# One pass of a decoder layer on Trainium2: in the last steps of the attention part VectorE makes norms and copies, weights come in order of use, pads go out on two queues

## The chip, the cores and the metric

The kernel runs on one core of one Trainium2 chip. The metric is the time of one execution on the device in microseconds (us). Engines are named as in the profile: PE (TensorE), DVE (VectorE), ACT (ScalarE), POOL (GpSimd) and SP (SyncE, which here only issues DMAs); PEld is PE's loading of weights.

## What is computed

A decoder layer with its norms behind each part, on x of 32 batches x 256 rows x 256 columns, all float32:

```python
x = _layernorm(x + _L0_attn_ref(x, Wq, Wk, Wv))               # 16 heads of 16, one k and v for all heads
x = _layernorm(x + _L0_xattn_ref(x, ctx, ctx, mask, W1, b1, W2, b2))   # 120 rows of context per batch
x = _layernorm(x + _L0_ffn_ref(x, Wg, W1, b1, Wo, bo))        # 8 experts, the two best per row
# in the last: comb holds the two best gate scores of a row, scaled to a sum of 1
for e in range(E):
    h = einsum('btd,hd->bth', x, W1[e]) + b1[e]
    a, b = split(h, 2)
    out = out + (einsum('bth,dh->btd', a * sigmoid(b), Wo) + bo) * comb[..., e:e + 1]
```

W1 has 8 experts of 1024 x 256, so one expert's weights are 1 MB.

## The kernel before

The program has three parts that follow each other.

**Attention** (function `attention`) is a software pipeline over the 32 batches, B = 32. A step t has 16 slots, u = 0 to 15; in each step the engines work on different stages of up to eight batches: t itself (projections), t-1 (maxima of the scores), t-3 (scores, exponentials, products with v), t-4 (transposes of attention's output, its sum with x, the statistics of norm 1), t-5 (norm 1, cross attention), t-6 (norm 2, the gate), t-7 (slots of the rows in the experts' lists, and POOL's indirect DMAs that write the rows there). Steps 0 to 31 bring in a batch each; steps 32 to 38 only drain. Every engine has its own program, written out by hand by slots, and works through it strictly in that order; semaphores tie the engines to each other. So an instruction that waits holds everything behind it on its engine.

The stages that matter here, for a batch b, with their lines:

- Step b+4: PE transposes attention's output in two halves, in slots 8 and 10 (`att_transpose`, L536, into the bank `psA`); DVE takes reciprocals and products (L849, L855), POOL adds x (L447), DVE makes statistics and moments (L833, L839). POOL then makes reciprocal root and shift (`rstd`, L408, L409, L411, L413).
- Step b+5: ACT applies norm 1 (L713, slot 0), PE transposes it (L563, slot 1), ACT copies that out of `psA` (L736, slot 2), PE multiplies with the keys (L579), DVE adds the mask and takes the maximum (L924, L928), ACT makes the exponentials (L759), PE transposes them (L612), ACT copies (L766), PE multiplies with the context (L628) and DVE finishes y2 (L1000, slot 14).
- Step b+6: DVE makes the moments of y2, POOL `rstd`, ACT norm 2 (L713, slot 4), PE transposes (L587), ACT copies out of the bank `psB` (L749, slot 6), PE scores the gate (L601), DVE works out the two best experts (L933 and what follows) and PE counts the rows per expert (L636 to L640).
- Step b+7: DVE makes the slots (L900, L907, L912), and POOL issues four indirect DMAs of rows (`dispatch`, L417).

The last steps also prepare the second part. SP loads the experts' weights in step 35, when the room of the probabilities is free (L288, `load_experts`), eight DMAs of 1 MB in the order of experts 0 to 7. ACT rounds each to `w1_hi` (`round_w1`, L684) and DVE makes the rest `w1_lo` (`split_w1`, L80), both in the order 4, 5, 6, 7, 0, 1, 2, 3 (`W1_ORDER`). Where these stand in the slots is set by two tables, (step, slot):

```python
rounds = {(B + 3, 15): W1_ORDER[0:2], (B + 4, 0): W1_ORDER[2:3], (B + 4, 7): W1_ORDER[3:4],
          (B + 4, 12): W1_ORDER[4:6], (B + 5, 7): W1_ORDER[6:7], (B + 5, 12): W1_ORDER[7:8]}
splits = {(B + 4, 3): 2, (B + 4, 6): 1, (B + 5, 3): 3}
```

**Experts** (function `experts`): DVE works out tables from the counts (L1367 to L1384): which rows and which expert each tile of 128 rows has. SP copies a pad of 128 rows behind each expert's list (L1161, eight DMAs), and then loads tiles (L1171). DVE makes the remaining pieces of `w1_lo` and `wo_lo` (L1388). PE waits for the tables and for all eight pieces; then a loop runs over 136 tiles: transposes (L1273), twelve matmuls (L1249, L1250, L1253), and on DVE, ACT and POOL the gating and the write of the result rows (L1405, L1412, L1416, L1329, L1212).

**Combination**: 32 pairs of tiles are read back, summed, multiplied with Wo, normed and stored.

## Time and profile before

| | |
|---|---|
| median of 3 executions | 1451.99 us (1448.6 to 1452.24) |
| the profiled execution, its own time | 1452.34 us |
| its span in the profile | 1449.7 us |
| busy: PE, DVE, ACT, POOL | 1272.7, 1129.4, 755.5, 639.0 us |
| steps 33 to 38 and the tables (754.1 to 864.4 us) | 110.3 us |
| tiles of the experts (864.4 to 1281 us) | about 417 us |

The profile describes one execution. A busy time counts an engine at work, the granted clock (PEclk) is the share of full speed at which PE was let run: 1.00 is 2.4 GHz, 0.50 is 1.2 GHz. Times of instructions are from the start of the span.

### The profile page before, as it was taken

Reading aid. Unit: us, or ns where it says so; the run is one execution under the profiler, and the core shown is the slowest. Engines: PE = TensorE matmul, PEld = TensorE weight load, DVE = VectorE, ACT = ScalarE, POOL = GpSimd, SP = SyncE. Lnnn points to the kernel's source line nnn. Section 1 sums busy time; section 2 is a strip of 40 time slices with the busy share of each in tenths; the row PEclk is TensorE's granted clock in tenths of the full one; section 3 lists DMA queues with packets and bytes.
Section 4 is the critical chain, followed back from the end, with each engine's and each line's share of the span. In section 5 each row is a group of like instructions: output and inputs, shape, how many; then the busy total and the mean of one; then the engine's idle time right before and its main releaser. Section 6 shows DMA issues by size and latency. Waiting matters only on the chain.

```text
span 1449.7 us, 29965 instructions
## 1 busy us (share of the span) xinstructions
PE 1272.7 (88%) x7668; PEld 895.3 (62%) x7669; DVE 1129.4 (78%) x3085; ACT 755.5 (52%) x1743; POOL 639.0 (44%) x1004
## 2 busy tenths in 40 slices
PE   6888999999999999999987429999999999968886
PEld 4443555655655555555543317888888888858786
DVE  1456788888888888888874567888888888859998
ACT  1125677777777777777777522222222222214444
POOL 3011244454455445445444343333333333348886
PEclk8999999999999999999999559999999999989999
DMA  6536456656556566566532843333334343369995
GB/s 163 108 62 103 80 106 130 126 116 131 124 118 130 122 120 131 121 121 130 120 83 74 329 145 112 133 133 132 131 132 132 132 132 132 131 261 320 335 337 195
DMA packets 171965, 212.75 MB, mean 147 GB/s; under 512 B 20064, under 2 KB 143072, under 8 KB 167648
## 3 DMA queue, kind: packets, MB, share of 16 engines
q1 hardware_dynamic: 148064, 145.01, 42.8%
q0 software_dynamic: 17568, 55.28, 10.2%
q10 hardware_dynamic: 6240, 11.34, 2.2%
q8 instruction: 44, 0.72, 0.2%
q14 instruction: 49, 0.40, 0.1%
HBM read 125.90 MB, written 85.98 MB: 146 GB/s over the span
## 4 chain that ended last, share of the span: by engine, by line
PE 59%; DVE 15%; issue 9%; ACT 7%; DMA 6%; SPq 2%; POOL 2%; DVEq 1%; ACTq 0%; POOLq 0%
PE psO L547 6%; PE psS L649 5%; PE psT L659 4%; PE psHb L1253 4%; PE psHb L1249 4%; PE psHb L1250 4%; PE psB L571 4%; PE psHa L1253 4%; PE psHa L1249 4%; PE psHa L1250 4%; DVE x2in L1447 3%; PE psO L502 2%; ACT x L713 2%; DVE gt_lo L1423 2%; PE psA L536 2%
## 5 line engine op out<-in xcount | busy, mean ns | idle before, releaser
L892 DVE TENSOR_REDUCE negmax<-psS 128x2 f32<-128x512 f32 x512 | 349.5, 687 | 98.2 <-PE psS L649 92.2
L791 ACT ACTIVATE probs<-psT 128x512 f32<-128x512 f32 x512 | 303.3, 598 | 168.4 <-PE psT L659 161.8
L1329 ACT ACTIVATE sig<-hb 128x512 f32<-128x512 f32 x136 | 86.1, 633 | 290.0 <-DVE hb L1405 290.0
L649 PE MATMUL psS<-kstack,qstack 96*128 96x256 bf16 x1024 | 194.9, 272 | 35.0 <-DVE kstack L988 14.2
L659 PE MATMUL psT<-qstack,kstack 99*128 99x512 bf16 x512 | 194.3, 381 | 5.1 <-ACT probs L791 5.1
L1212 POOL DMA_INDIRECT g_rows<-g,slot x136 | 135.4, 996 | 70.4 <-issue 66.6
L649 PEld LDWEIGHTS psS<-kstack,qstack 96*128 96x128 bf16 x1024 | 92.3, 104 | 92.0 <-DVE negmax L892 34.8
L417 POOL DMA_INDIRECT lists<-x,slots x128 | 128.1, 1001 | 34.1 <-issue 30.2
L547 PE MATMUL psO<-probs,vaug 128*32 128x512 f32 x1024 | 139.0, 615 | 0.9 <-ACT probs L791 0.8
L1405 DVE TENSOR_TENSOR hb<-psHb,b 128x512 f32<-128x512 f32 x136 | 94.1, 692 | 38.0 <-issue 34.1
L1416 DVE SCALAR_TENSOR_TENSOR g<-g,xe,sig 128x512 f32<-128x512 f32 x136 | 102.2, 752 | 25.9 <-DVE g L1412 17.0
L1249 PE MATMUL psHb<-w_hi,xet_hi 128*128 x272 | 119.0, 438 | 0.0
L447 POOL TENSOR_TENSOR y<-att,xres 128x512 f32<-128x512 f32 x32 | 40.3, 1259 | 163.3 <-DVE att L855 163.3
L1207 POOL TENSOR_TENSOR away<-xe,expf 128x1 f32<-128x1 f32 x136 | 24.6, 181 | 197.5 <-DVE g L1416 186.8
L1249 PE MATMUL psHa<-w_hi,xet_hi 128*128 x272 | 107.9, 397 | 0.0
L1250 PE MATMUL psHb<-w_lo,xet_hi 128*128 x272 | 107.9, 397 | 0.0
L1250 PE MATMUL psHa<-w_lo,xet_hi 128*128 x272 | 107.3, 395 | 0.0
L1412 DVE TENSOR_TENSOR g<-psHa,b 128x512 f32<-128x512 f32 x136 | 93.9, 691 | 9.2 <-PE psHa L1253 7.0
L430 POOL TENSOR_TENSOR qpart<-qrest,one_c 128x512 bf16<-128x512 f32 x32 | 33.3, 1040 | 148.5 <-DVE qrest L917 148.5
L1223 POOL TENSOR_TENSOR row_sum<-rows 128x512 f32<-128x512 f32 x64 | 86.6, 1375 | 9.8 <-DMA rows<-g_rows 8.5
L1338 ACT CAST gt_hi<-psHa 128x512 fp32r<-128x512 f32 x64 | 37.6, 587 | 94.4 <-PE psHa L1305 94.4
L1253 PE MATMUL psHa<-w_hi,xet_lo 128*128 x272 | 86.1, 397 | 0.0
(195 smaller groups left out, 2934.1 us busy)
## 6 DMA issues: line engine op xcount, KB each, us to landing
rows<-g_rows SPq DMA_DIRECT2D x32, 1024.0 KB, 8.1
qstack<-q_parts SPq DMA_DIRECT2D x192, 128.0 KB
xe<-lists SPq DMA_DIRECT2D x136, 133.0 KB, 2.1
q_parts<-qpart SPq DMA_DIRECT2D x32, 384.0 KB, 2.8
sums<-x SPq DMA_DIRECT2D x32, 264.0 KB, 2.3
x2in<-sums SPq DMA_DIRECT2D x32, 264.0 KB, 4.9
xt<-in_x_t SPq DMA_DIRECT2D x32, 256.0 KB, 6.4
xres<-in_x SPq DMA_DIRECT2D x32, 256.0 KB, 3.2
```

The source lines that it names most:

```text
L417: pool.indirect_dma_start(out=dram["lists"], out_offset=bass.IndirectOffsetOnAxis(ap=slots[:, b.s2, 2 * c + k:2 * c + k + 1], axis=0), in_ ...
L547: last = mm(psO[32 * i:32 * i + 32, g, :], vaug[:, b.s4, kc, :], probs[:, (4 * w + i) % PT, :], start=kc == 0, stop=kc == 1)
L649: last = mm(psS[:, u % 2, hh * S:(hh + 1) * S], qstack[0:KROWS, b1.s4, 2 * hp + hh, c * P:(c + 1) * P], kstack[0:KROWS, b1.s4, :], start=T ...
L659: mm(psT[:, u % 2, :], kstack[0:KROWS + MROWS, b3.s4, kc * P:(kc + 1) * P], heads, start=True, stop=True).then_inc(sm["scored"], 1)
L791: nc.scalar.activation(probs[:, u % PT, :], psT[:, u % 2, :], ACT.Exp, scale=SELF_SCALE).then_inc(sm["exp_done"], 1)
L892: v.tensor_reduce(negmax[:, b1.s2, 2 * hp:2 * hp + 2, c], psS[:, u % 2, :].rearrange("p (h k) -> p h k", h=2), AX.X, ALU.max, negate=True) ...
L1212: pool.indirect_dma_start(out=dram["g_rows"], out_offset=bass.IndirectOffsetOnAxis(ap=slot[:, o.s4:o.s4 + 1], axis=0), in_=g[:, o.s4], in_ ...
L1249: mm(out, hi[:, part], w_hi(k), start=k == 0, stop=False)
L1250: mm(out, hi[:, part], w_lo(k), start=False, stop=False)
L1253: last = mm(out, lo[:, k * P:(k + 1) * P], w_hi(k), start=False, stop=k == chunks - 1)
L1405: v.tensor_tensor(hb[:, i.s2], psHb[:, i.s2, :], b1[:, bass.ds(e * H2 + H, H)], ALU.add).then_inc(sm["hb_ready"], 1)
L1416: v.scalar_tensor_tensor(g[:, i.s4], g[:, i.s4], xe[:, i.s4, bass.ds(e + D, 1)], sig[:, i.s2], ALU.mult, ALU.mult).then_inc(sm["g_ready"], 1)
```

## The change

In the steps behind step 32 (`draining(t)`, steps 33 to 38) the work is dealt out anew:

- Norm 1 and norm 2 are applied by DVE (`own_norm`), norm 1 already in slot 11 of step b+4, norm 2 in slot 3 of step b+6. DVE also makes variance plus epsilon and the shift (`own_rstd`); POOL keeps only the power (`power`). DVE copies the transposed rows out of `psA` and `psB` (x1t in slot 2, x2t in slot 6).
- PE transposes attention's output in slots 0 and 4 and in a bank of its own (`psS`), and DVE's reciprocals, products and statistics move up to slots 0, 1, 4, 5, 8 and 9.
- The weights are loaded in the order of use. ACT rounds three pieces at the end of step 35, two in slot 7 and three in slot 12 of step 36. DVE makes three pieces of `w1_lo` in slot 6 of step 36 and one in slot 6 of step 37; four are left for behind the tables.
- At the end of step 37 PE makes 80 matmuls of 128 x 128 whose result nobody reads (`keep_busy`).
- The pads are copied by SP (experts 0 to 3) and ACT (4 to 7).
- The tables and the loop cover 135 tiles in place of 136, and the last six rounds of the tiles' pipeline are written out where three were.

```diff
+    def draining(t):
+
+        return t.n > B
+
+    def att_bank(t, g):
+
+        return psS[:, g] if draining(t) else psA
+
...
-                for e in range(E):
+                for e in W1_ORDER:
                     sp.dma_start(dram["w1_raw"][:, dram["piece"](e)].rearrange("p (c h) -> p c h", c=DC),
                                  io["f1_t"][e].rearrange("(c p) h -> p c h", p=P)
...
+        def power(b, vare, out, ready):
+
+            wait(pool, ready, 3 * b.n + 1)
+            pool.tensor_tensor(out[:, b.s2], vare[:, b.s2], neg_half[:, :], ALU.pow).then_inc(sm[ready], 1)
+
...
+            if active(b6) and draining(t):
+                power(b6, vare2, rstd2, "rstd2_ready")
+            elif active(b6):
                 rstd(b6, "var2_ready", mv2, vare2, nmean2, rstd2, shift2, "rstd2_ready")
             if active(t):
...
-                rstd(b4, "var1_ready", mv1, vare1, nmean1, rstd1, shift1, "rstd1_ready",
-                     ("score_link", done(b4.back(2))))
+                if draining(t):
+                    power(b4, vare1, rstd1, "rstd1_ready")
+                    wait(pool, "score_link", done(b4.back(2)))
+                else:
+                    rstd(b4, "var1_ready", mv1, vare1, nmean1, rstd1, shift1, "rstd1_ready",
...
-            bank_read(bank_a, t, f"att_transposed{g}")
+            if draining(t):
+                wait(pe, "max_reduced", UNITS * B)
+                wait(pe, "att_normed", 2 * b.n + g - 1)
+            else:
+                bank_read(bank_a, t, f"att_transposed{g}")
             for c in range(QC):
                 for hh in range(2):
-                    last = nc.tensor.transpose(psA[:, (c * 2 + hh) * P:(c * 2 + hh + 1) * P],
+                    last = nc.tensor.transpose(att_bank(t, g)[:, (c * 2 + hh) * P:(c * 2 + hh + 1) * P],
...
+        def keep_busy(count):
+
+            for _ in range(count):
+                mm(psS[:, 0, 0:P], all_ones[:, :], before[:, :], start=True, stop=True)
...
-                if u == 8 and active(b4):
+                if u == (0 if draining(t) else 8) and active(b4):
                     att_transpose(t, 0)
-                if u == 10 and active(b4):
+                if u == (4 if draining(t) else 10) and active(b4):
                     att_transpose(t, 1)
...
+            if t.n == B + 5:
+                keep_busy(80)
...
-        rounds = {(B + 3, 15): W1_ORDER[0:2], (B + 4, 0): W1_ORDER[2:3], (B + 4, 7): W1_ORDER[3:4],
-                  (B + 4, 12): W1_ORDER[4:6], (B + 5, 7): W1_ORDER[6:7], (B + 5, 12): W1_ORDER[7:8]}
+        rounds = {(B + 3, 15): W1_ORDER[0:3], (B + 4, 7): W1_ORDER[3:5], (B + 4, 12): W1_ORDER[5:8]}
...
-                if u == 0 and active(b5):
+                if u == 0 and active(b5) and not draining(t.back(1)):
                     wait(act, "y2_ready", done(b5.back(2)))
...
                     wait(act, "x1_transposed", done(b5))
                     wait(act, "cross_scored", done(b5.back(2)))
                     copy(x1t[:, b5.s2].rearrange("p c s -> p (c s)"), psA[:, :]).then_inc(sm["x1t_copied"], 1)
...
-        splits = {(B + 4, 3): 2, (B + 4, 6): 1, (B + 5, 3): 3}
+        splits = {(B + 4, 6): 3, (B + 5, 6): 1}
...
-            return psA[:, :].rearrange("p (c j k) -> p c j k", c=QC, k=32), rden[:, g].rearrange("p (c j) -> p c j", c=QC)
+            return att_bank(Step(0, b.n + 4), g).rearrange("p (c j k) -> p c j k", c=QC, k=32), rden[:, g].rearrange("p (c j) -> p c j", c=QC)
...
 
+        def own_rstd(b, mv, vare, out, shift, var, ready, k):
+
+            if k == 0:
+                wait(dve, var, done(b))
+                v.tensor_scalar(vare[:, b.s2], mv[:, b.s2, :, 1], EPS, None, ALU.add).then_inc(sm[ready], 1)
+            else:
+                wait(dve, ready, 3 * b.n + 2)
+                v.scalar_tensor_tensor(shift[:, b.s2], mv[:, b.s2, :, 0], -1.0, out[:, b.s2], ALU.mult, ALU.mult
+                                       ).then_inc(sm[ready], 1)
+
+        def own_norm(x, rs, shift, y, b, ready, name):
+
+            wait(dve, ready, done(b, 3))
+            for c in range(QC):
+                last = v.tensor_scalar(x[:, b.s2, c, 0:D], y[:, b.s2, c, :], rs[:, b.s2, c:c + 1], shift[:, b.s2, c:c + 1],
+                                       ALU.mult, ALU.add)
+            last.then_inc(sm[name], 1)
+
+        def drain_slot(t, u):
+
+            b4, b5, b6 = t.back(4), t.back(5), t.back(6)
+            if active(b4):
+                if u == 0:
+                    att_reciprocal(b4, 0)
+                if u == 1:
+                    att_norm(b4, 0)
+            if active(b6):
+                if u in (2, 3):
+                    own_rstd(b6, mv2, vare2, rstd2, shift2, "var2_ready", "rstd2_ready", u - 2)
+                if u == 3:
+                    wait(dve, f"x2_stored{b6.s2}", 16 * b6.half)
+                    wait(dve, "x2_transposed", done(b6.back(2)))
+                    wait(dve, f"dispatched{b6.s2}", 2 * QC * 16 * b6.half)
+                    own_norm(x2, rstd2, shift2, y2, b6, "rstd2_ready", "x2_ready")
+            if active(b5) and u == 2:
+                wait(dve, "x1_transposed", done(b5))
+                wait(dve, "cross_scored", done(b5.back(2)))
+                v.tensor_copy(x1t[:, b5.s2].rearrange("p c s -> p (c s)"), psA[:, :]).then_inc(sm["x1t_copied"], 1)
+            if active(b6) and u == 6:
+                wait(dve, "x2_transposed", done(b6))
+                wait(dve, "gate_scored", done(b6.back(2)))
+                v.tensor_copy(x2t[:, b6.s2].rearrange("p c s -> p (c s)"), psB[:, :]).then_inc(sm["x2t_copied"], 1)
+            if active(b4):
+                if u == 4:
+                    att_reciprocal(b4, 1)
+                if u == 5:
+                    att_norm(b4, 1)
+                if u == 8:
+                    wait(dve, "y1_ready", done(b4))
+                    stats(y1, stats1, b4, "stats1_ready")
+                if u == 9:
+                    wait(dve, "stats1_ready", done(b4))
+                    moments(stats1, mv1, b4, "var1_ready")
+                if u in (10, 11):
+                    own_rstd(b4, mv1, vare1, rstd1, shift1, "var1_ready", "rstd1_ready", u - 10)
+                if u == 11:
+                    wait(dve, "y2_ready", done(b4.back(2)))
+                    wait(dve, "x1_transposed", done(b4.back(2)))
...
     STRIDE = dram["stride"]
-    TILES = 2 * T // P + E
+    TILES = 2 * T // P + E - 1
...
                 step(Step(j, r))
-        for r in range(3):
+        for r in range(TILES % 4 + 3):
             step(Step(TILES // 4, r))
 
     def pair_pipeline(eng, step):
...
 
+    def copy_pads(eng, lists):
+
+        eng.wait_ge(dram["pads_stored"], 32)
+        eng.wait_ge(sm["pads_placed"], 1)
+        for e in lists:
+            row = eng.value_load(pad_tab[0:1, e:e + 1], min_val=0, max_val=(E - 1) * STRIDE + T)
+            eng.dma_start(dram["lists"][bass.ds(row, P), :], dram["pad_rows"][e * P:(e + 1) * P, :]
+                          ).then_inc(sm["pads_written"], 16)
+
     def sync(sp, drained):
-        sp.wait_ge(dram["pads_stored"], 32)
-        sp.wait_ge(sm["pads_placed"], 1)
-        for e in range(E):
-            row = sp.value_load(pad_tab[0:1, e:e + 1], min_val=0, max_val=(E - 1) * STRIDE + T)
-            sp.dma_start(dram["lists"][bass.ds(row, P), :], dram["pad_rows"][e * P:(e + 1) * P, :]
-                         ).then_inc(sm["pads_written"], 16)
+        copy_pads(sp, range(0, E // 2))
         drained(sp)
         sp.wait_ge(sm["tables_ready"], 2)
         sp.wait_ge(sm["pads_written"], 16 * E)
...
-            sp.wait_ge(sm[f"g_stored{s}"], 16 * (TILES // 4))
+            sp.wait_ge(sm[f"g_stored{s}"], 16 * ((TILES - s + 3) // 4))
 
         def pair_step(t):
...
         copy = nc.scalar.copy
+        copy_pads(act, range(E // 2, E))
         act.wait_ge(dram["wo_loaded"], 16)
         copy(wo_hi[:, :, :], wo_raw[:, :, :]).then_inc(dram["wo_rounded"], 1)
```

**ACT, end of step 35 and start of step 36.** `x<-y` is a norm, `w_hi` the rounding of a piece of W1, `x1t` the copy of transposed rows. Before:

```order
L773 ACTIVATE gtop<-top,gneg 128x2
L684 CAST w_hi<-w_raw 128x2048 [waits pads_stored,w1_loaded4]
L684 CAST w_hi<-w_raw 128x2048 [waits w1_loaded5]
L713 ACTIVATE x<-y,shift,rstd 128x256 [waits rstd1_ready,x1_transposed,y2_ready]
L713 ACTIVATE x<-y,shift,rstd 128x256
L684 CAST w_hi<-w_raw 128x2048 [waits w1_loaded6]
L736 COPY x1t<-psA 128x512 [waits cross_scored,x1_transposed]
```

Now:

```order
L802 ACTIVATE gtop<-top,gneg 128x2
L714 CAST w_hi<-w_raw 128x2048 [waits pads_stored,w1_loaded4]
L714 CAST w_hi<-w_raw 128x2048 [waits w1_loaded5]
L714 CAST w_hi<-w_raw 128x2048 [waits w1_loaded6]
L788 ACTIVATE cprob,csum<-cscore,cnegmax 128x120 [waits y2_ready,cprob_transposed,cross_masked]
```

The norm and the copy that stood behind the roundings are gone from ACT; the exponentials of cross attention come next.

**DVE, step 36, from the last step of the slots to the gate's scores.** Before:

```order
L912 CAST slots<-slotf 128x4 [waits slot_link]
L80 TENSOR_TENSOR w_lo<-w_raw,w_hi 128x2048 [waits w1_rounded] x2
L924 SCALAR_TENSOR_TENSOR cscore<-psA,mask_b 128x240 [waits mask_ready,cross_exp,cross_scored]
L928 TENSOR_REDUCE cnegmax<-cscore 128x2 [waits score_link]
L80 TENSOR_TENSOR w_lo<-w_raw,w_hi 128x2048 [waits w1_rounded]
L933 COPY logits<-psB 128x16 [waits gate_exp,gate_scored]
```

Now:

```order
L908 TENSOR_SCALAR vare<-mv 128x2 [waits var2_ready]
L941 COPY x1t<-psA 128x512 [waits cross_scored,x1_transposed]
L911 SCALAR_TENSOR_TENSOR shift<-mv,rstd 128x2 [waits rstd2_ready]
L918 TENSOR_SCALAR x<-y,rstd,shift 128x256 [waits dispatched0,rstd2_ready,x2_transposed,x2_stored0]
L918 TENSOR_SCALAR x<-y,rstd,shift 128x256
L1015 SCALAR_TENSOR_TENSOR cscore<-psA,mask_b 128x240 [waits mask_ready,cross_exp,cross_scored]
L1019 TENSOR_REDUCE cnegmax<-cscore 128x2 [waits score_link]
L945 COPY x2t<-psB 128x512 [waits gate_scored,x2_transposed]
L80 TENSOR_TENSOR w_lo<-w_raw,w_hi 128x2048 [waits w1_rounded] x3
L1024 COPY logits<-psB 128x16 [waits gate_exp,gate_scored]
```

The five instructions of the norm and the copies came in, with waits for POOL and for DMAs, and all three pieces now stand between x2t and the logits.

**DVE, step 37, the same stretch.** Before:

```order
L839 BN_AGGR mv<-stats 128x2 [waits stats2_ready]
L907 TENSOR_REDUCE slotf<-chosen 128x4 [waits slot_link]
L912 CAST slots<-slotf 128x4 [waits slot_link]
L80 TENSOR_TENSOR w_lo<-w_raw,w_hi 128x2048 [waits w1_rounded] x3
L933 COPY logits<-psB 128x16 [waits gate_exp,gate_scored]
```

Now:

```order
L1001 CAST slots<-slotf 128x4 [waits slot_link]
L908 TENSOR_SCALAR vare<-mv 128x2 [waits var2_ready]
L911 SCALAR_TENSOR_TENSOR shift<-mv,rstd 128x2 [waits rstd2_ready]
L918 TENSOR_SCALAR x<-y,rstd,shift 128x256 [waits dispatched1,rstd2_ready,x2_transposed,x2_stored1]
L918 TENSOR_SCALAR x<-y,rstd,shift 128x256
L945 COPY x2t<-psB 128x512 [waits gate_scored,x2_transposed]
L80 TENSOR_TENSOR w_lo<-w_raw,w_hi 128x2048 [waits w1_rounded]
L1024 COPY logits<-psB 128x16 [waits gate_exp,gate_scored]
```

Three pieces ahead of the norm became one behind it. Behind the tables (L1384 before, L1480 now) two pieces stood, and now four.

## Rows read from the trace of the kernel before

**Rows 1.** Windows: steps 33, 34 and 35; columns in the first line.

```profile
core 0: us, PE busy (x) PEld busy (x) DVE busy (x) ACT busy (x) POOL busy (x), PEclk, DMA share, GB/s
754.10:771.82 17.72, 13.88 (x92) 6.70 (x92) 9.11 (x45) 14.18 (x37) 8.40 (x14) 1.00 0.22 71
771.82:792.30 20.48, 16.41 (x93) 7.39 (x85) 8.03 (x43) 13.90 (x36) 8.36 (x14) 0.83 0.18 59
792.30:807.38 15.08, 9.88 (x51) 6.96 (x51) 7.95 (x42) 5.81 (x18) 6.54 (x10) 0.67 0.93 343
```

**Rows 2.** Timeline, start of step 36: start, duration, engine, line, operation, [idle before <-releaser].

```profile
813.08 1.90 ACT L684 CAST w_hi<-w_raw 128x2048 fp32r<-128x2048 f32 x1 [10.88 <-DMA w_raw<-in_f_t]
...
817.05 1.09 ACT L713 ACTIVATE x<-y,shift,rstd 128x256 f32<-128x256 f32 x2
...
818.19 1.11 PE L563 MATMUL psA<-ident,x 128*128 128x128 f32 x4 [12.27 <-ACT x L713]
```

**Rows 3.** Timeline, further in step 36.

```profile
820.42 0.58 ACT L736 COPY x1t<-psA 128x512 f32<-128x512 f32 x1
...
821.09 2.03 PE L579 MATMUL psA<-keymap,x1t 128*128 128x120 f32 x8 [1.79 <-ACT x1t L736]
...
827.17 0.66 PE L612 MATMUL psB<-ident,cprob 128*120 128x128 f32 x2 [0.52 <-issue]
...
830.48 0.88 DVE L1000 SCALAR_TENSOR_TENSOR y<-psA,crec,x 128x256 f32<-128x256 f32 x2 [0.71 <-PE psA L628]
```

**Rows 4.** Timeline, a power in step 34, and step 37.

```profile
789.56 0.72 POOL L411 TENSOR_TENSOR rstd<-vare,neg_half 128x2 f32<-128x2 f32 x1
...
833.08 6.68 DVE L80 TENSOR_TENSOR w_lo<-w_raw,w_hi 128x2048 fp32r<-128x2048 f32 x3
...
835.49 2.65 POOL L411 TENSOR_TENSOR rstd<-vare,neg_half 128x2 f32<-128x2 f32 x1
...
839.93 1.09 ACT L713 ACTIVATE x<-y,shift,rstd 128x256 f32<-128x256 f32 x2 [7.16 <-POOL shift L413]
...
844.89 0.17 DVE L933 COPY logits<-psB 128x16 f32<-128x16 f32 x1 [5.14 <-PE psB L601]
```

**Rows 5.** Timeline, tables, pads, pieces and the first tile.

```profile
848.35 0.17 DVE L1367 CAST pad_tab<-base 128x8 int32<-128x8 f32 x1
...
849.82 9.60 SPq L1161 DMA_DIRECT2D lists<-pad_rows  x8
...
855.89 4.49 DVE L80 TENSOR_TENSOR w_lo<-w_raw,w_hi 128x2048 fp32r<-128x2048 f32 x2
...
862.12 16.99 SPq L1171 DMA_DIRECT2D xe<-lists  x7
...
864.41 0.66 PE L1273 MATMUL psX<-ident,xe 128*128 128x128 f32 x2 [17.60 <-DMA xe<-lists]
```

**Rows 6.** The tiles' transposes, two of them a tile: ns min/median/max, first and last start.

```profile
L1273 PE MATMUL psX<-ident,xe x272: 270/272/476, 864.4 to 1273.5; 128*128 128x128 f32 x136
```

**Rows 7.** DMA issues from 798 to 808 us: KB each, us to landing.

```profile
sums<-x SPq DMA_DIRECT2D x1, 264.0 KB, 15.1
lists<-x,slots POOLq DMA_INDIRECT x2, 6.4
```

**Rows 8.** Windows behind the last tile; columns as in rows 1.

```profile
1278.00:1280.00 2.00, 1.41 (x7) 0.79 (x5) 1.46 (x4) 0.39 (x1) 0.97 (x1) 1.00 0.24 88
...
1282.00:1283.00 1.00, 0.00 (x0) 0.00 (x0) 0.17 (x1) 0.00 (x0) 0.45 (x1) 0.53 1.07 321
```

**Rows 9.** Timeline, POOL's sum and a short DVE operation beside it.

```profile
785.44 1.26 POOL L447 TENSOR_TENSOR y<-att,xres 128x512 f32<-128x512 f32 x1 [8.58 <-DVE att L855]
785.49 1.25 DVE L965 TENSOR_TENSOR hotsum<-hot 128x16 bf16<-128x16 f32 x1
```

**Rows 10.** Timeline, the same eight matmuls at the two clocks.

```profile
771.29 1.07 PE L547 MATMUL psO<-probs,vaug 128*32 128x512 f32 x8
...
778.36 1.94 PE L547 MATMUL psO<-probs,vaug 128*32 128x512 f32 x8
```

More of the change, by code:

```diff
@@ L732, in step @@
                     copy_att(b4, 1)
-                if u == 2 and active(b5):
+                if u == 2 and active(b5) and not draining(t):
                     wait(act, "x1_transposed", done(b5))
@@ L942, in step @@
                     last.then_inc(sm["gate_max"], 1)
-                if u == 8 and active(b4):
+                if u == 8 and active(b4) and not draining(t):
                     att_norm(b4, 0)
@@ L948, in step @@
                     last.then_inc(sm["gate_link"], 1)
-                if u == 10 and active(b4):
+                if u == 10 and active(b4) and not draining(t):
                     att_reciprocal(b4, 1)
```

21 lines of the change are left out of this document (12 added, 9 removed).

## Prediction, made before the changed kernel was run

> **What bounds the kernel now.** The windows over the program's parts show which engine limits each. Over the tiles of the experts PE works without a gap: the 136 tiles' transposes start between 864.4 and 1273.5 us, (1273.5 - 864.4) / 135 = 3.03 us a tile [rows 6]. That stage and the combination behind it are untouched by the change, but for one tile. What it changes is the drain of attention, steps 33 to 38 and the tables, 754.1 to 864.4 us, where no engine is full: windows by step, then the timeline step by step, tell what each step waits for.
>
> In steps 33 and 34 PE works 13.88 of 17.72 and 16.41 of 20.48 us, ACT some 14 in both, DVE 9.11 and 8.03 [rows 1]: PE is first, and its gaps are short waits for ACT, so DVE has room and ACT little. Then the last batch, 31, goes alone from stage to stage. In step 36 its norm 1 stands on ACT behind two roundings whose pieces of W1 are the fifth and sixth of eight loads: ACT sits idle 10.88 us for the first, the norm starts at 817.05, and PE has waited 12.27 us for it [rows 2]. In step 37 its norm 2 needs four small POOL operations, which run beside three w_lo pieces on DVE; the power takes 2.65 us there and 0.72 alone, ACT waits 7.16 us for the shift, and the gate's logits come at 844.89 [rows 4]. Last, the pads occupy SP from 849.82 for 9.60 us, the first tile is asked for at 862.12, and PE starts at 864.41, 4.0 us after the last of the w_lo pieces (855.89 + 4.49 = 860.38) [rows 5].
>
> **The change, part by part.** I follow batch 31.
>
> *Norm 1 off ACT, loads in order of use.* Step 35 closes at 807.38 [rows 1]. Now the norm stands in DVE's slot 11 of step 35, with attention's transposes moved up so that y1 is there in time; DVE has 7.95 of 15.08 us to do there, so I leave the step's length, less 0.6 for the transposes that no longer wait in slot 10: 806.8. PE transposes x1 at once, hidden behind DVE's statistics of y2. On DVE: statistics, moments and slots 1.3 (807.45 to 808.75 in the timeline of before), variance and x1t 0.8: no row has that copy on DVE, ACT's takes 0.58 [rows 3], a DVE operation out of the same banks 0.69; I take 0.6. At 808.9 PE can score, 2.03 [rows 3], then mask and maximum 0.9, x2t 0.7: 812.6. ACT is not in the way: it needs the first three loads. The fifth landed just ahead of 813.08 and the first, by the shortest landing of 8.3 us from 793.9, at 802.2, so 2.7 apart; the third comes at 807.6 and its rounding ends near 809.5. Norm 2 of batch 30 stands ahead of the mask on DVE and waits for the writes of batch 28: issued by about 802, 6.4 us to landing [rows 7], 808.5, just in time.
>
> *Three pieces in slot 6.* 3 x 2.28 = 6.8 us of DVE, on the path, since the logits (and through the bank psB all that PE does next) stand behind them: 819.5. Their cover was the wait for the loads, and it is gone. From the transposes of the exponentials to the end of y2 it takes 827.17 to 831.36, 4.2 us [rows 3], with 0.2 for the logits 4.4: y2 ends at 823.9 against 831.36. **Gain 7.4.**
>
> *Norm 2 in step 37.* Before, 831.36 to 844.89, 13.5 us [rows 3, 4]. Now: comb, statistics and moments 1.5 as before; variance 0.2, POOL's power 0.72 [rows 4] with nothing beside it, shift 0.2, two norms. These have no row on DVE: ACT's pair takes 1.09 [rows 4], DVE's statistics of the same 256 elements 0.41 each; between 0.3 and 1.1 I take 0.8, near the statistics. With 0.2 of hops 3.6 in all. Then transposes 1.1, x2t 0.6, and one piece, 2.28, beside the gate's matmuls (1.85): 7.8. **Gain 5.7.** The copies of rows to the lists and the sums are not late: the store that queues behind the loads took 15.1 us [rows 7], so it is there at 822.5, needed at 826.
>
> *Four pieces behind the tables in place of two.* Slots, pad_tab and tables take as long as before. Two pieces more, 2 x 2.25 [rows 5], all on the path: **loss 4.5.**
>
> *Pads on two queues.* SP's 9.60 us become 4.8, the other half runs on ACT beside it. All is 13.1 earlier (7.4 + 5.7): SP starts at 836.7, its last pad lands some 2.8 after issue at 843.8, the last rows of POOL's dispatch at about 845; a tile can be there at 847.4. DVE's last piece ends at 860.38 - 13.1 + 4.5 = 851.8. So the wait for the tile is covered, **gain 4.0**, and what is late next is DVE with its pieces, 4.4 us ahead of the next in line.
>
> *Steps 33 and 34.* ACT loses two norms and two copies a step, 2 x 1.09 + 2 x 0.58 = 3.3 us, and DVE takes them in its room. What of it reaches the path is between nothing (PE was waiting for its own order) and all of PE's idle time, 3.8 + 4.1 = 7.9 us [rows 1]. PE's waits with an ACT release sum to some 3.9 in step 33 and somewhat less in step 34; I take a third of both steps' idle: **gain 2.5.**
>
> *The 80 matmuls* start behind the last counts, near 835, and have ended by some 845 at the latest (two of 256 columns took 0.38 at full clock in the timeline), so they delay nothing, and PE then stands idle until 851.8. Behind the last tile the granted clock is 1.00 in the window of PE's last matmuls and 0.53 in the window from 1282, with nothing between [rows 8]. So I give them **0**; if they held the clock, the first tile would cost about 2 us less. The Trainium skill (TensorE: Matmul & The Clock Gate, What's actually happening) says that activity releases the throttle and idleness brings it back; by that rule too such matmuls pay only if they run up to the first tile, and 2 us would come off the sum if they did.
>
> *One tile less*: **3.0** [rows 6]. Writing out six rounds costs instructions, not work.
>
> Sum: 7.4 + 5.7 - 4.5 + 4.0 + 2.5 + 0 + 3.0 = 18.1. The profiled execution took 1452.34, which gives **1434 us**; the median of the runs, 1451.99, lies 0.35 below it, within what a measurement can tell (0.3%, 4.4 us). The bounds of this case alone: 5.4 more if all of PE's idle time went, 2.5 less if none, and 2 less if the norms cost as on ACT: 1429 to 1439.
>
> **The rivals.**
>
> *POOL holds up DVE's new operations.* A hotsum of 0.17 us took 1.25 while POOL added y [rows 9]. The new shift and norms work on SBUF too, beside POOL's dispatches and its sum. For it: norm 1 and norm 2 of each step fall among four dispatches. Against it: in steps 36 and 37 POOL has no y to add, and the statistics beside dispatches kept 0.74 a pair. Price: four waits of about 1 us on batch 31's path and the 2.5 of steps 33 and 34, 6.5: **1441.** The Trainium skill (SBUF — State Buffer, Who interferes with whom) has it that VectorE, reading two SBUF inputs or in a two-port mode, and GpSimd lock each other out for a whole instruction; by that rule a norm would wait for a dispatch that began first, and this is the rival's time.
>
> *DVE hangs in slot 3 of step 36 on the writes of batch 28.* The loads fill the DMA engines (share 0.93 in step 35 [rows 1]). If those rows land with the last load, near 821, in place of 808.5, mask, splits and y2 all shift: y2 at 834.5 in place of 823.9, 10.6 less: **1445.** Against it: 6.4 us was measured in that very stretch.
>
> *All goes better*: PE's gaps close (5.4) and the clock stays up (2): **1427.**
>
> *Gain only from the tile*: DVE, in order, holds up PE in steps 33 to 35 by its waits for POOL's power in slots 3 and 11, and what batch 31 wins is lost there: 1452.3 - 3.0 = **1449**, no difference that can be told.
>
> *Slower: the clock falls early.* It is 1.00 in step 33, 0.83 and 0.67 in the next two [rows 1]; eight matmuls took 1.07 and 1.94 us at the two levels [rows 10]. If PE's work in another rhythm lets the clock fall to 1.2 GHz at the start of step 33, PE's 13.88 us become 25, 7 to 11 longer than the step allows; step 34 has the same work and loses 5 to 8; step 35 2. Up to 21, with the 2.5 gone: 1434 + 23.5 = **1458.** It decides only if half clock holds through both steps. Against it: PE's share of work rises if its gaps close, and steps 33 and 34 keep 15 to 16 us of PE busy.
>
> **How the numbers follow.** Forecast 0.55, POOL 0.14, the writes 0.12, all better 0.10, only the tile 0.05, slower 0.04. The first four are faster by over 0.3%: 0.91; same 0.05; slower 0.04. The range takes in the forecast's bounds, the better case and the two partial ones: 1427 to 1446.
>
> **What would show it.** Right: x1's last transposes near 806 to 810 and not behind a rounding; three w_lo pieces in one block ahead of the logits; POOL's power at about 0.7 in step 37; four pieces between the tables and the first tile, and PE's first transpose then, 849 to 852, waiting for DVE and not for a DMA; steps 33 and 34 together 2 to 3 us shorter; 135 tiles at 3.03. Wrong: norms of 1 us and more on DVE beside dispatches; DVE idle on a DMA in step 36; a first tile at full clock; tiles at another pace; or a start of the tiles later than 858.

## The result, and the profile after

| | before | after |
|---|---|---|
| median of the runs, us | 1451.84 (1448.6 to 1452.24) | 1431.34 (1423.52 to 1440.3) |
| profiled execution, us | 1452.34 | 1429.97 |
| its span, us | 1449.7 | 1428.1 |

The ratio is 0.9861, with a 95% interval from 0.9831 to 0.989: faster, by 20.5 us of the medians where 18 was forecast. The same kernel in a second set of runs, e0 below, has a median of 1430.34 and a profiled execution of 1426.37.

The windows of the changed kernel, cut where DVE's update of base closes a step, as in [rows 1], with steps 36 and 37 added:

```profile
core 0: us, PE busy (x) PEld busy (x) DVE busy (x) ACT busy (x) POOL busy (x), PEclk, DMA share, GB/s
756.31:773.22 16.91, 14.51 (x99) 6.86 (x97) 10.70 (x57) 11.93 (x31) 7.32 (x8) 1.00 0.23 73
773.22:789.41 16.19, 13.63 (x92) 6.50 (x92) 10.49 (x52) 11.59 (x29) 7.32 (x8) 1.00 0.22 75
789.41:802.30 12.89, 7.25 (x49) 4.78 (x50) 10.34 (x53) 5.02 (x14) 7.33 (x8) 0.86 0.89 327
802.30:819.64 17.34, 8.39 (x35) 6.55 (x33) 14.35 (x44) 11.80 (x17) 6.18 (x5) 0.50 1.03 404
819.64:829.70 10.06, 4.07 (x27) 3.61 (x28) 7.49 (x36) 3.84 (x8) 5.62 (x5) 0.50 1.03 408
```

Steps 33 to 35 took 17.72, 20.48 and 15.08 us [rows 1] and take 16.91, 16.19 and 12.89. Some 2 us of work a step went from ACT to DVE. And the granted clock, 1.00, 0.83 and 0.67 before, is now 1.00, 1.00 and 0.86: PE does step 34 in 13.63 busy us in place of 16.41.

The timeline of steps 36 and 37 after (start, duration, engine, line, operation, idle before and its releaser), which answers to [rows 2 to 4]:

```profile
801.84 1.90 ACT L714 CAST w_hi<-w_raw 128x2048 fp32r<-128x2048 f32 x1 [1.14 <-DMA w_raw<-in_f_t]
...
802.03 1.09 PE L591 MATMUL psA<-ident,x 128*128 128x128 f32 x4 [1.06 <-DVE y L1091]
...
803.64 0.68 DVE L941 COPY x1t<-psA 128x512 f32<-128x512 f32 x1
...
804.85 0.97 DVE L918 TENSOR_SCALAR x<-y,rstd,shift 128x256 f32<-128x256 f32 x2
...
807.96 6.68 DVE L80 TENSOR_TENSOR w_lo<-w_raw,w_hi 128x2048 fp32r<-128x2048 f32 x3
...
818.35 0.88 DVE L1091 SCALAR_TENSOR_TENSOR y<-psA,crec,x 128x256 f32<-128x256 f32 x2 [0.71 <-PE psA L656]
...
821.16 0.72 POOL L426 TENSOR_TENSOR rstd<-vare,neg_half 128x2 f32<-128x2 f32 x1 [10.09 <-DVE vare L908]
...
822.22 0.74 DVE L918 TENSOR_SCALAR x<-y,rstd,shift 128x256 f32<-128x256 f32 x2
...
824.77 2.28 DVE L80 TENSOR_TENSOR w_lo<-w_raw,w_hi 128x2048 fp32r<-128x2048 f32 x1
826.97 0.17 DVE L1024 COPY logits<-psB 128x16 f32<-128x16 f32 x1
```

PE transposes batch 31's x1 at 802.03, as step 35 closes (802.30), and not 10.8 us behind its end as before (818.19 against 807.38). ACT waits for its loads beside it and nobody waits for ACT. The three pieces stand in one block ahead of the logits, and POOL's power takes 0.72 us in step 37, not 2.65.

Tables, pads, pieces and the first tile after, for [rows 5]:

```profile
828.75 6.52 PE L577 MATMUL psS<-before,all_ones 128*128 128x128 bf16 x80
...
830.41 0.16 DVE L1463 CAST pad_tab<-base 128x8 int32<-128x8 f32 x1
...
832.08 5.49 SPq L1253 DMA_DIRECT2D lists<-pad_rows  x4
...
837.92 8.89 DVE L80 TENSOR_TENSOR w_lo<-w_raw,w_hi 128x2048 fp32r<-128x2048 f32 x4
...
841.06 3.71 SPq L1266 DMA_DIRECT2D xe<-lists  x4
...
846.91 0.66 PE L1368 MATMUL psX<-ident,xe 128*128 128x128 f32 x2 [11.65 <-DVE w_lo L80]
```

PE's first transpose now waits for DVE's last piece and not for a DMA, as forecast. The tile was asked for at 841.06; POOL, which waited for it, had it by 843.31. For [rows 6]:

```profile
L1368 PE MATMUL psX<-ident,xe x270: 270/272/473, 846.9 to 1252.1; 128*128 128x128 f32 x135
```

That makes (1252.1 - 846.9) / 134 = 3.02 us a tile.

The ledger of the two profiled executions, in us:

| stretch | before | after | gain | forecast |
|---|---|---|---|---|
| start to end of step 32 | 754.10 | 756.31 | -2.2 | 0 |
| steps 33 and 34 | 38.20 | 33.10 | 5.1 | 2.5 |
| step 35 | 15.08 | 12.89 | 2.2 | 0.6 |
| step 36 | 24.39 | 17.34 | 7.05 | 6.8 |
| step 37 up to pad_tab | 16.58 | 10.77 | 5.8 | 5.7 |
| pad_tab to the first tile | 16.06 | 16.50 | -0.4 | -0.5 |
| tiles' first to last transpose | 409.1 | 405.2 | 3.9 | 3.0 |
| last transpose to the end | 176.2 | 176.0 | 0.2 | 0 |

The gains sum to 21.6, the difference of the spans. The end of step 32 lies between 752.5 and 761.4 in the fourteen profiled executions of this study, whatever the kernel, the tail is 175.6 to 176.4 in all, and the tiles take 402.9 to 405.5 in the ten with 135 of them: the largest part of the scatter arises ahead of anything that the change touches. So parts are compared below by the lengths of steps, which repeat within 0.1 us in e0 (16.91, 16.19, 12.88, 17.35, 10.07) against the first execution. Steps 33 to 35 do not always repeat so well. Seven executions share the changed kernel's code there; in three of them (e2, e11, e12) the clock fell in step 33, which took 18.3 to 18.5 us, and in e1 and e2 step 35 took 13.3. A difference of that size in one profile is therefore no effect by itself:

```profile
756.53:774.84 18.31, 15.93 (x96) 7.51 (x94) 10.70 (x57) 11.79 (x31) 7.32 (x8) 0.91 0.22 67
```

(step 33 of e2.)

### The profile page after: what moved, and what is told of

Read it like the earlier page. It is cut to its first block and busy times, and to the rows that moved or that the text cites. A ratio compares the mean times of both kernels' runs of the same rounds, so it can differ in the third digit from the quotient of the medians.

```text
span 1428.1 us, 29996 instructions
## 1 busy us (share of the span) xinstructions
PE 1272.3 (89%) x7734; PEld 898.8 (63%) x7735; DVE 1136.6 (80%) x3121; ACT 742.4 (52%) x1716; POOL 635.3 (44%) x978
## 5 line engine op out<-in xcount | busy, mean ns | idle before, releaser
L1302 POOL TENSOR_TENSOR away<-xe,expf 128x1 f32<-128x1 f32 x135 | 27.8, 206 | 192.1 <-DVE g L1512 185.0
L1348 PE MATMUL psHb<-w_hi,xet_lo 128*128 x270 | 85.1, 396 | 0.0
```

The lines of the kernel that those rows point to most:

```text
L1348: last = mm(out, lo[:, k * P:(k + 1) * P], w_hi(k), start=False, stop=k == chunks - 1)
```

## The experiments

Twelve kernels, in three groups, each group with its own runs of the kernel before on the same chip (medians 1452.63, 1451.88 and 1452.24).

**e0, the changed kernel again**, as the group's own yardstick.

> The changed kernel once more, as the yardstick on this chip. In its first profile steps 33 to 38 and the tables took 90.6 us (754.1 to 864.4 before: 110.3), and the tiles began 17.5 us earlier in the span although step 32 had ended 2.2 us later; its four times lay between 1423.5 and 1440.3. If that spread comes from the drain, the 90.6 will differ here by several us; if it comes from the start of the program or the combination, the 90.6 stays within 0.5 and the end of step 32 (756.3) or the part behind the last tile (176.0 us) moves.

Measured: 1430.34 us (1426.37 to 1432.17), ratio 0.9844 (0.979 to 0.9897). From step 32's end to the first tile 90.6 us, as in the first execution; step 32 ended 1.6 earlier and the tiles took 1.5 less.

**e1, without the 80 matmuls.**

```
-            if t.n == B + 5:
-                keep_busy(80)
```

> The changed kernel without the 80 matmuls at the end of step 37. Theory: they bring nothing, since PE idles 11.6 us behind them and the first tile ran at half clock with them (first to second pair of transposes behind the start 6.4 us, as in the kernel before): same start of the tiles, same first tile, ratio to the kernel before as for the changed kernel within noise. Rival: they keep something warm all the same, and the first tiles get 1 to 2 us longer without them.

Measured: 1427.1 us (1425.04 to 1431.37), ratio 0.9818 (0.9761 to 0.9875). From pad_tab to the first tile 16.52 us against 16.50 (16.51 in e0), from the first to the third tile's transposes 6.52 against 6.44 (5.13 in e0). They bring nothing that these runs can show. The granted clock of the changed kernel behind them shows why; windows:

```profile
833.00:835.00 2.00, 2.00 (x40) 2.00 (x38) 1.93 (x3) 0.00 (x0) 1.69 (x2) 1.00 0.83 208
837.00:839.00 2.00, 0.00 (x0) 0.00 (x0) 1.97 (x3) 0.24 (x1) 0.00 (x0) 1.00 0.88 311
839.00:841.00 2.00, 0.00 (x0) 0.00 (x0) 2.00 (x2) 0.00 (x0) 0.00 (x0) 0.64 0.03 11
...
848.00:850.00 2.00, 2.00 (x6) 1.62 (x7) 0.85 (x2) 1.43 (x2) 0.00 (x0) 0.50 0.00 0
```

The matmuls end at 835.3, PE stands idle for 11.65 us, and the first tiles run at half clock (0.63 us for a matmul that takes 0.40 later).

**e2, 140 matmuls more, right up to the first tile.** Their results are read by nobody.

```
+        some = ident[:, :].bitcast(mybir.dt.bfloat16)[:, 0:P]
+        for _ in range(140):
+            mm(psX[:, 0, 0:P], some, some, start=True, stop=True)
```

> The changed kernel with 140 more matmuls of 128 x 128 in bfloat16, nobody reads them, between PE's wait for the tables and its wait for the pieces of W1. In the profile of the changed kernel the granted clock is 1.00 up to 839 us and 0.79 in the next, and the tables end at 838.0, so these begin while it is full; at the 0.06 us that one of the 80 took at full clock they last 8.4 of the 8.9 us until the last piece. Theory: PE enters the first tile at 2.4 GHz, and the span from its first transposes to the fourth pair (846.9 to 856.4, 9.5 us) shrinks by 2 us: about 2 us faster than the changed kernel. Rival: matmuls on a matrix of ones and zeros do not hold the clock, or they overrun the last piece by up to 2 us: no gain or 2 us slower.

Measured: 1426.47 us (1424.32 to 1430.11), ratio 0.9808 (0.9754 to 0.9862). PE's timeline and two windows:

```profile
840.35 7.99 PE L1340 MATMUL psX<-ident 128*128 128x128 bf16 x140 [2.70 <-DVE exp_tab L1483]
849.16 0.44 PE L1371 MATMUL psX<-ident,xe 128*128 128x128 f32 x2 [0.81 <-DVE w_lo L80]
...
850.53 0.39 PE L1348 MATMUL psHb<-w_lo,xet_hi 128*128 x1
```

```profile
847.00:849.00 2.00, 1.34 (x25) 1.17 (x21) 2.00 (x1) 0.00 (x0) 1.84 (x1) 1.00 0.52 131
849.00:851.00 2.00, 1.42 (x8) 1.08 (x9) 1.76 (x4) 0.86 (x3) 1.29 (x2) 1.00 0.00 0
```

The clock stays at 1.00, and the first to third tile take 3.93 us in place of 5.1 to 6.5: 1.2 to 2.6 us less, which the prediction put at about 2. The runs' times can't tell e2 from e1 or e0, since their ranges overlap.

**e6, the copies x1t and x2t back on ACT**, all else as changed.

```
-                if u == 2 and active(b5) and not draining(t):
+                if u == 2 and active(b5):
...
-                if u == 6 and active(b6) and not draining(t):
+                if u == 6 and active(b6):
```

(and the two copies out of `drain_slot`)

> The changed kernel with the copies of transposed rows (x1t, x2t) back on ACT in steps 33 to 38, all else as changed. Theory: 2 x 0.58 us more on ACT a step stand between its exponentials and lengthen steps 33 and 34 together by 1 to 2 us; in step 36 the x1 copy waits behind three roundings, which end at 806.6, against 803.6 for DVE's copy: 3 us later there, the pieces then start 3 us later; 4 to 5 us slower than the changed kernel in all. Rival: the copies are hidden wherever they are, and steps 33 to 35 stay within 0.5 us; then the gain there came from the norms and the earlier transposes alone.

Measured: 1433.88 us (1432.97 to 1435.58), ratio 0.9868 (0.9814 to 0.9921). Steps 33 to 37 are longer by 0.7, 1.6, 0.1, 1.5 and 0.1: 4.0 in all, near the 4 to 5 that was expected. But the clock was not the same. Windows of its steps 33 and 34:

```profile
754.92:772.53 17.61, 14.75 (x98) 6.80 (x97) 9.39 (x55) 12.90 (x33) 7.32 (x8) 1.00 0.21 70
772.53:790.30 17.77, 15.09 (x89) 7.36 (x90) 9.28 (x50) 12.44 (x31) 7.31 (x8) 0.91 0.21 68
```

The 0.7 of step 33 stands at full clock. The 1.6 of step 34 stands at 0.91, and a fall to 0.91 alone cost step 33 as much in e2, e11 and e12. So of 2.4 us in steps 33 to 35 only 0.7 is shown to be the copies'.

**e3, before with one tile less.**

```
-    TILES = 2 * T // P + E
+    TILES = 2 * T // P + E - 1
```

(and the loops' ends that follow from it)

> The kernel before with 135 tiles in place of 136 and its last rounds written out, nothing else. All rows still have a tile. Theory: one tile's 3.03 us less, everything else equal. Rival: the written-out rounds or shorter tables give more (the changed kernel's span from first to last transposes is 3.9 us shorter than before, not 3.0), then 4 us; or the last tile was covered by the stores behind it and the gain is below 1 us.

Measured: 1446.87 us (1445.31 to 1449.3), ratio 0.9967 (0.9947 to 0.9986). First to last transpose took 405.1 us against 409.1 (407.4 to 409.1 in the four executions with 136 tiles), so the 3.03 of the tile is borne out and no more than that can be told. The windows of its steps 33 to 35 are of use beyond that:

```profile
754.68:775.05 20.37, 16.45 (x87) 7.59 (x87) 8.62 (x47) 13.68 (x36) 8.40 (x14) 0.83 0.19 62
775.05:793.34 18.29, 14.30 (x98) 6.72 (x98) 8.55 (x43) 14.80 (x37) 8.38 (x14) 1.00 0.21 67
793.34:807.13 13.79, 8.13 (x51) 5.57 (x43) 7.95 (x42) 5.45 (x18) 6.54 (x10) 0.76 0.94 347
```

The code of these steps is that of before, yet the low clock fell in step 33 here, which took 20.37 us, and step 34 took 18.29. So a stretch at the lower level costs a step some 2.2 to 2.7 us, and wanders. Step 35 is 1.3 shorter than before, and step 36 is 25.83 us long where it was 24.39: together 39.62 against 39.47.

**e4, before with W1 loaded in order of use.**

```
-                for e in range(E):
+                for e in W1_ORDER:
```

> The kernel before with the eight loads of W1 in order of use, nothing else. Theory: the first rounding starts at about 802 in place of 813.08 and norm 1 of the last batch at about the time its shift is ready (808.7) in place of 817.05; the two pieces of w_lo in slot 3 of step 36 then stand on the path, 4.5 us, and the norm 2 of step 37 stays slow (POOL beside three pieces): the tiles start 3 to 5 us earlier than in the kernel before. Rival: the load order alone gives all of step 36's 7 us, and moving norm 1 to DVE nothing.

Measured: 1443.51 us (1441.02 to 1446.48), ratio 0.9926 (0.9899 to 0.9952). Timeline of its step 36:

```profile
810.43 4.99 DVE L80 TENSOR_TENSOR w_lo<-w_raw,w_hi 128x2048 fp32r<-128x2048 f32 x2
...
810.59 1.09 ACT L713 ACTIVATE x<-y,shift,rstd 128x256 f32<-128x256 f32 x2 [2.74 <-POOL shift L413]
...
811.74 1.11 PE L563 MATMUL psA<-ident,x 128*128 128x128 f32 x4 [4.05 <-ACT x L713]
```

ACT now waits for POOL's shift and not for a load. Step 36 takes 17.78 us in place of 24.39: the order alone gives 6.6, nearly all of what the whole change gives there (7.05), and more than was expected: the rival held. DVE makes its two pieces (810.43 to 815.42) while the norm, its transposes and the scoring go on elsewhere, and the mask behind them waits another 0.70 us for PE; so the pieces are not on the path, where the expectation had them.

**e5, before with pads on two queues.** The loop of SP becomes `copy_pads(sp, range(0, E // 2))`, and ACT begins with

```
+        copy_pads(act, range(E // 2, E))
```

> The kernel before with the pads on SP and ACT, four each, nothing else. Theory: the first tile is there by 859, PE starts behind the last piece at 860.5 in place of 864.4: 4 us less. Rival: the drain of POOL's rows or the DMA engines set the first tile's load, and it moves by less than 2 us.

Measured: 1447.19 us (1445.15 to 1450.23), ratio 0.9965 (0.9948 to 0.9982). SP, DVE and PE in its timeline:

```profile
850.11 4.54 SPq L1162 DMA_DIRECT2D lists<-pad_rows  x4
...
856.18 4.49 DVE L80 TENSOR_TENSOR w_lo<-w_raw,w_hi 128x2048 fp32r<-128x2048 f32 x2
...
859.25 3.71 SPq L1175 DMA_DIRECT2D xe<-lists  x4
...
861.50 0.66 PE L1277 MATMUL psX<-ident,xe 128*128 128x128 f32 x2 [14.38 <-DMA xe<-lists]
```

From pad_tab to the first tile 12.86 us against 16.06: 3.2, not the 4.0 that the pieces would allow, because the tile's load (asked for at 859.25) still ends last, 0.8 behind DVE (860.67). In the changed kernel DVE has four pieces there, and is last.

**e7, before with three small matmuls in each slot of steps 33 to 35**, results unread.

```
+                if t.n in (B + 1, B + 2, B + 3):
...
+                    for _ in range(3):
+                        mm(psS[:, 0, 0:P], all_ones[:, :], before[:, :], start=True, stop=True)
```

> The kernel before with three matmuls of 128 x 128 in bfloat16, read by nobody, ahead of each slot's score in steps 33 to 35, nothing else. It asks why steps 34 and 35 became 4.4 and 2.2 us shorter in the changed kernel, more than forecast. Granted clock: 0.83 and 0.67 before, 1.00 and 0.86 changed. Theory: the clock is a cause, PE's own work at 1.2 GHz held these steps up; with filler the clock stays at 2.4 GHz and steps 34 and 35 get shorter by 2 to 4 us together although PE has 3 x 16 x 0.06 = 2.9 us more a step to do. Rival: the removed waits alone did it and the clock followed; then these steps get no shorter, or longer by up to 3 us each.

Measured: 1451.36 us (1445.67 to 1456.77), ratio 0.9983 (0.9965 to 1.0002). Windows of steps 33 to 35:

```profile
758.04:777.57 19.53, 17.25 (x145) 9.82 (x148) 9.12 (x47) 14.24 (x36) 8.40 (x14) 1.00 0.20 65
777.57:796.58 19.01, 16.36 (x142) 9.52 (x138) 8.53 (x43) 14.47 (x36) 8.37 (x14) 1.00 0.19 64
796.58:810.20 13.62, 9.27 (x96) 7.33 (x88) 7.94 (x41) 5.49 (x18) 6.54 (x10) 0.97 0.91 337
```

With more work for PE, steps 34 and 35 got 2.9 us shorter (35.56 to 32.63), at a clock of 1.00 and 0.97 where it was 0.83 and 0.67; step 33, at 1.00 in both, paid 1.8 for the filler. So the clock is a cause of these steps' length. The drain as a whole did not get shorter: step 36 took 26.24 us, 1.85 more, and from the end of step 32 to pad_tab it took 94.99 us against 94.25. The loads of W1 are issued 1.2 us behind the start of step 35, and with the old order step 36 waits for them, so what step 35 gains step 36 gives back: 39.86 us for the two, against 39.47 before, 39.62 in e3 and 39.63 in e5.

**e9, the changed kernel with W1 loaded in the old order.**

```
-                for e in W1_ORDER:
+                for e in range(E):
```

> The changed kernel with W1 loaded in the order 0 to 7 again; the roundings keep their order of use. Theory (load order is what shortened step 36: alone it gave 6.6 us there): the pieces that ACT's first roundings and DVE's three w_lo pieces ask for are then the fifth, sixth and seventh loads, so the roundings wait until some 816 us, batch 31's cross attention waits behind them on ACT, step 36 is 6 to 10 us longer than the changed kernel's 17.3, and the time about 1437 to 1441. Rival (norm 1 on DVE alone frees step 36, the order is a detail): step 36 within 2 us of 17.3, the time within 2 us of the changed kernel.

Measured: 1435.69 us (1434.74 to 1436.92), ratio 0.9882 (0.985 to 0.9914). Step 36 takes 24.14 us, 6.8 more, all other steps are within 0.02. ACT's timeline:

```profile
810.01 1.90 ACT L714 CAST w_hi<-w_raw 128x2048 fp32r<-128x2048 f32 x1 [11.60 <-DMA w_raw<-in_f_t]
```

Norm 1 was in time (x1's transposes at 801.67), but the exponentials of cross attention and the three pieces waited behind the loads. The theory held; off ACT, the norm is worth nothing in step 36 alone if the loads come in the old order. Steps 35 and 36 together take 37.02 us, against 39.47 before and 30.23 in the changed kernel.

**e10, the changed kernel with both norms back on ACT**, variance and shift back on POOL.

```
-            if active(b6) and draining(t):
-                power(b6, vare2, rstd2, "rstd2_ready")
-            elif active(b6):
+            if active(b6):
...
-                if u == 0 and active(b5) and not draining(t.back(1)):
+                if u == 0 and active(b5):
...
-                if u == 4 and active(b6) and not draining(t):
+                if u == 4 and active(b6):
```

(norm 1's POOL part likewise, and own_rstd and own_norm out of `drain_slot`)

> The changed kernel with both norms back on ACT and their variance and shift back on POOL behind step 33; transposes, copies, load order, pads as changed. Theory (the prediction's account: step 37 was shortened by norm 2 on DVE, its chain through POOL being the cost; step 36 mostly by the load order): step 37 longer by 2 to 4 us, step 36 longer by 1 to 5 (norm 1 behind ACT's three roundings), steps 33 and 34 together by 1 to 3; in all 5 to 10, time 1436 to 1441. Rival (POOL's chain costs nothing once no three w_lo pieces run beside it, so that step 37's gain came from moving the pieces to slot 6): step 37 within 1 us of 10.06, and the time within 4 us of the changed kernel.

Measured: 1436.0 us (1432.12 to 1437.43), ratio 0.9888 (0.9855 to 0.992). Timeline:

```profile
804.07 2.07 ACT L736 ACTIVATE x<-y,shift,rstd 128x256 f32<-128x256 f32 x4
...
805.21 1.12 PE L585 MATMUL psA<-ident,x 128*128 128x128 f32 x4 [8.11 <-ACT x L736]
...
810.69 6.68 DVE L80 TENSOR_TENSOR w_lo<-w_raw,w_hi 128x2048 fp32r<-128x2048 f32 x3
```

Step 36 takes 23.97 us, 6.6 more, above the 1 to 5 that was expected: the norm stands behind three roundings, x1's transposes come 6.8 us behind the end of step 35, and DVE's three pieces, which e4 had in slot 3 beside that wait, are now queued behind it. Step 37 takes 10.54, only 0.5 more: there the rival held, though the time of the whole kernel came out in the theory's range. Steps 33 and 34 take 1.1 more, at a clock of 1.00 in both. Step 35, where the norm of batch 31 no longer stands, takes 1.2 less.

**e11, half pieces.** W1's low part is made in sixteen pieces of 1024 columns, six of them behind the tables.

```
-        splits = {(B + 4, 6): 3, (B + 5, 6): 1}
+        splits = {(B + 4, 6): 6, (B + 4, 11): 1, (B + 5, 4): 1, (B + 5, 6): 2}
```

> The changed kernel with W1's low part made in sixteen half pieces in place of eight whole ones: six behind slot 6 of step 36, one behind slot 11, one behind slot 4 of step 37 and two behind slot 6, where DVE waits for others, six behind the tables. Theory (DVE's pieces are what the first tile waits for): DVE ends its last piece 2 us earlier, the tiles start 1.5 to 2.3 us earlier, time 1428 to 1430. Rival (what fills DVE's waits delays the gate's logits or norm 2 by as much): the start of the tiles moves by less than 0.7 us.

Measured: 1429.98 us (1425.92 to 1431.3), ratio 0.9832 (0.9802 to 0.9862). Timeline:

```profile
841.49 6.89 DVE L83 TENSOR_TENSOR w_lo<-w_raw,w_hi 128x1024 fp32r<-128x1024 f32 x6
...
848.48 0.66 PE L1373 MATMUL psX<-ident,xe 128*128 128x128 f32 x2 [9.97 <-DVE w_lo L83]
```

From pad_tab to the first tile 14.50 us against 16.50, 2.0 less, but steps 36 and 37 are 0.2 and 0.6 longer. The start gains 1.2 us: between theory and rival.

**e12, half pieces and 105 bridging matmuls** (the edits of e11 and e2, with `range(105)`).

> Half pieces as in the run before, and 105 matmuls of 128x128 bf16 on PE between its wait for the tables and its wait for the last low piece, whose results nobody reads. Theory (both act, on different terms: DVE's pieces 2 us, the clock over the first tiles 2 us): granted clock 1.00 over the first tiles, first to third tile's transposes 4 us apart and not 5 to 6.5, time about 4 us under the changed kernel, 1425 to 1427. Rival (matmuls outlast DVE's earlier end, or the clock falls in between): at most 2 us under the changed kernel.

Measured: 1427.97 us (1425.74 to 1434.24), ratio 0.9827 (0.9799 to 0.9855). PE's timeline:

```profile
845.62 7.66 PE L1345 MATMUL psX<-ident 128*128 128x128 bf16 x105 [2.97 <-DVE exp_tab L1488]
853.12 0.39 PE L1376 MATMUL psX<-ident,xe 128*128 128x128 f32 x2
```

First to third tile 3.86 us, so the clock held, but the matmuls outlast DVE (852.38) by 0.7 us. From pad_tab to the third tile it takes 19.0 us (20.4 in e2, 20.0 in e11, 21.6 to 23.0 without either). The parts add, less the 0.7 and the 0.8 that steps 36 and 37 give back; that the matmuls outlast DVE was the rival's condition. The best median of all is e2's, but e0, e1, e2, e11 and e12 lie within 3.9 us of each other, on two chips, and these runs don't tell them apart.

## Why the prediction was right, point by point

**The mechanism was right** and so was its order: norm 1 no longer late, pieces in one block, power at 0.72, DVE last before the first tile, 135 tiles at 3.02. The terms of step 36 (6.8 against 7.05), step 37 (5.7 against 5.8), the two pieces (4.5 against 4.4), the pads (4.0: the first tile starts 0.4 later behind pad_tab with 4.4 more of pieces) and the tile (3.0; 3.9 in the ledger, of which about 1 is scatter, the pace having been 3.03 and 3.02) all held within a microsecond. The profiled execution ended 4.3 under the sum (1434.2): 4.2 more than forecast in steps 33 to 35, about 0.9 more in the tiles and 0.6 in the other terms, less 2.2 by which step 32 ended later, makes 3.5, and the rest lies outside the span. That the number came so close is in part luck: the later end of step 32, which is scatter, hid half of the mis-sized term. One small slip in the working: the items listed for step 37 add to 7.6 us, not 7.8, which would have made that gain 5.9.

**The term that was mis-sized: steps 33 to 35.** "I take a third of both steps' idle: gain 2.5" and 0.6 for step 35; measured 5.1 and 2.2, 4.2 more in all. The upper bound on the two steps was PE's idle time, 7.9, and the trace keeps within it, but the step failed in what it was a bound of: PE's busy time was taken as fixed. It fell from 16.41 to 13.63 us in step 34, mostly since the clock stayed at 1.00 (14.30 in e3, where the old code ran that step at 1.00). The term had no part for the clock, and the rows at both levels show how large that part is. At a clock of 1.00 step 33 took 17.72 us before and takes 16.91; step 34 took 18.29 in the kernel before's code (e3) and takes 16.19. That is 2.9 where 2.5 was forecast. Step 35 took 13.79 at 0.76 (e3) and 13.3 at 0.74 in the changed kernel's code (e1, e2): 0.5 where 0.6 was forecast. The remaining 3.9 of the 7.3 goes with the higher clock, 2.2 in step 34 and 1.7 in step 35. So work moved off ACT gave what was said, and the clock was left out. These are comparisons of single profiles. Of the 2.9, the norms off ACT account for 1.1 (e10) and the copies for 0.7 in step 33 (e6); the rest, for the copies in step 34 and for attention's transposes in slots 0 and 4, was not tried: no run moved the transposes alone. Why the clock stays up is not shown either. And it does not hold for certain: it was 0.91 in step 33 of e2, e11 and e12, which took 1.4 to 1.6 us more.

**Step 36 was summed rightly, but its causes were told as one.** The heading was "Norm 1 off ACT, loads in order of use". The order alone gives 6.6 (e4), and without it the change gives nothing there (e9: 24.1 us). All that the change has beside the order adds 0.44 to e4's step 36, and yet taking the norms back costs 6.6 there (e10). Both are true, since DVE's pieces sit in slot 3 in e4, where they cover the norm's wait, and in slot 6 in the changed kernel, where they follow it. Steps 35 and 36 together are the fairer measure, since the loads are issued in step 35: 39.47 before, 32.86 with the order alone (e4), 37.02 with all but the order (e9), 35.65 with all but the norms (e10), 30.23 with all. "Their cover was the wait for the loads, and it is gone" was right; its counterpart, that with the order alone cover and pieces would stay, was not seen.

**Step 37's 5.7 came for another reason than the new place of norm 2.** With the norms on ACT it is 10.54 long against 15.86 before (e10): what counts, by elimination, is that not three pieces but one stand in it, behind the transposes and not beside POOL's power; no run moved the pieces alone. The order of loads gives nothing there (15.86 in e4), the norm on DVE 0.5, the copies 0.1 (e6). The two pieces are paid behind the tables, 4.4, where the pads had left 4.0 of room.

**The rivals.** *POOL holds up DVE*: the mechanism is there and is small. A pair of norms takes 0.97 us in step 36 and 0.74 in step 37, both beside a dispatch that began 0.15 before it (804.69 and 822.07, 1.04 us each). A shift takes 0.65 in step 35 in place of 0.16, and ends as POOL's work on a mask ends (798.96 to 799.64). A dispatch that falls in with the pieces takes 2.50 us, not 0.96:

```profile
799.01 0.65 DVE L911 SCALAR_TENSOR_TENSOR shift<-mv,rstd 128x2 f32<-128x2 f32 x1 [0.47 <-POOL rstd L426]
...
807.31 0.96 POOL L430 DMA_INDIRECT lists<-x,slots  x1 [0.30 <-issue]
808.57 2.50 POOL L430 DMA_INDIRECT lists<-x,slots  x1 [0.30 <-issue]
```

Four waits of about 1 us were priced; those on batch 31's path sum to under 1. The Trainium skill (SBUF — State Buffer, Who interferes with whom) has VectorE, with two SBUF inputs or in a two-port mode, and GpSimd lock each other out for a whole instruction. The shift and the 2.50 us beside the pieces agree with that; the norms at 0.74 to 0.97 beside dispatches show that a dispatch did not hold them up for its whole length. *The writes of batch 28*: wrong; DVE's norm at 804.85 follows the shift at once. *All goes better*: in part, the clock in steps 33 to 35 stayed up, that over the first tiles did not (e1 agrees with the 0 for the 80 matmuls, and e2 with the 2 us that they could give: 1.2 to 2.6). The Trainium skill (TensorE: Matmul & The Clock Gate, What's actually happening) says that idleness brings the throttle back; the first tiles agree, at 0.50 behind 11.65 us of idle PE and at 1.00 in e2. *Only the tile* is excluded by the ledger, where the tiles start 17.5 us earlier, and by e3 (1446.87). *Slower, the clock falls early*: it did not in this execution; where it fell in step 33 (e2, e11, e12) the price was 1.4 to 1.6 us, not 20.
